# A transformer block on one core: weighted values ahead of scores in two steps, another order of GpSimd's last groups, x transposes one by one, more banks for the last group

## What is computed

```
qkv = x @ w_qkv.T + b_qkv                       # x is [4, 512, 512]
scores = q @ k.T / sqrt(32) + causal            # per head
out = softmax(scores) @ v
x = layernorm(x + out @ w_out.T + b_out)
W = (w_int - 128) * scale                       # gate, up, down
h = silu(x @ Wg.T) * (x @ Wu.T)
x = layernorm(x + h @ Wd.T)
```

## Time and profile before

| | us |
|---|---|
| median of 3 runs | 764.74 (764.24 to 765.97) |
| profiled execution | 766.57 |
| its span, first to last instruction | 764.4 |

### The profile page before, as it was taken

One profiled execution on the slowest core, in us unless ns is written; L12 is line 12 of the kernel. 1 busy time (PEld: TensorE's weight loads), 2 busy tenths in 40 slices (PEclk: granted clock), 3 DMA queues, 4 the chain that ended last, 5 costly groups with the idle time before them and its releaser, 6 DMA issues.

```text
span 764.4 us, 11953 instructions
## 1 busy us (share of the span) xinstructions
PE 739.4 (97%) x4480; PEld 567.4 (74%) x4480; DVE 393.2 (51%) x1004; ACT 382.7 (50%) x912; POOL 135.6 (18%) x154
## 2 busy tenths in 40 slices
PE   7999899999999999999799999999999999999995
PEld 6776676776776677776478887888887888788884
DVE  3757566566666665676643222553226432363335
ACT  3656767666767666766646565322323222322230
POOL 0000111314221151300736222220000000000003
PEclk9999999999999999999999999999999999999998
DMA  9201422334531355211586964541110011000201
GB/s 318 95 1 29 138 64 75 83 85 110 166 84 56 83 153 158 50 56 56 127 145 145 200 226 138 167 138 41 69 56 0 9 51 49 0 1 27 83 1 57
DMA packets 59463, 68.67 MB, mean 90 GB/s; under 512 B 33552, under 2 KB 35600, under 8 KB 59280
## 3 DMA queue, kind: packets, MB, share of 16 engines
q1 hardware_dynamic: 52880, 48.00, 20.7%
q0 software_dynamic: 6528, 19.93, 11.1%
HBM read 59.53 MB, written 14.68 MB: 97 GB/s over the span
## 4 chain that ended last, share of the span: by engine, by line
PE 90%; DVE 4%; POOL 3%; ACT 2%; DMA 1%; issue 0%; POOLq 0%; SPq 0%; DVEq 0%
PE bank L1425 15%; PE bank L1424 15%; PE bank L1210 12%; PE bank L1286 9%; PE bank L1431 7%; PE bank L1432 7%; PE bank L1225 6%; PE bank L1269 5%; PE bank L1244 5%; PE bank L1307 5%; DVE probs L968 1%; POOL z_tok L643 1%; PE bank L1318 1%; PE bank L1182 1%; PE bank L1172 1%; PE bank L1393 1%
## 5 line engine op out<-in xcount | busy, mean ns | idle before, releaser
L752 ACT ACTIVATE probs<-probs,neg_max 128x128 f32<-128x128 f32 (+3 forms) x256 | 140.4, 553 | 12.2 <-DVE neg_max L968 12.2
L1084 DVE SCALAR_TENSOR_TENSOR hid<-bank,u_scale,silu 128x512 f32<-128x512 f32 x64 | 48.0, 751 | 166.9 <-PE bank L1425 165.7
L968 DVE CUSTOM_DVE_ANT_0 probs<-bank,causal 128x128 f32<-128x128 f32 (+3 forms) x256 | 111.7, 484 | 29.4 <-PE bank L1269 28.2
L1424 PE MATMUL bank<-xT_hi,gateT 128*128 128x512 f32 x256 | 100.3, 392 | 0.0
L1425 PE MATMUL bank<-xT_lo,gateT 128*128 128x512 f32 x256 | 99.7, 389 | 0.0
L1424 PE MATMUL bank<-xT_hi,upT 128*128 128x512 f32 x256 | 99.6, 389 | 0.0
L1425 PE MATMUL bank<-xT_lo,upT 128*128 128x512 f32 x256 | 99.6, 389 | 0.0
L860 ACT ACTIVATE silu<-bank,g_scale 128x512 f32<-128x512 f32 x64 | 44.0, 687 | 99.6 <-PE bank L1425 99.6
L804 ACT ACTIVATE probsT<-bank 128x512 f32<-128x512 f32 x80 | 47.7, 597 | 90.0 <-PE bank L1286 89.8
L1286 PEld LDWEIGHTS bank<-ident,probs 128*128 128x128 f32 x640 | 73.3, 141 | 26.1 <-issue 15.4
L1431 PE MATMUL bank<-downT,hid_hi 128*128 128x512 f32 x232 | 90.6, 390 | 0.9 <-DVE hid_lo L1088 0.8
(11 more groups left out here) (102 smaller groups left out, 1165.3 us busy)
## 6 DMA issues: line engine op xcount, KB each, us to landing
scan_buf<-in_L_ffn_gate_w_dram SPq DMA_DIRECT2D x4, 1024.0 KB, 5.1
scan_buf<-in_L_ffn_up_w_dram SPq DMA_DIRECT2D x4, 1024.0 KB, 5.0
scan_buf<-in_L_ffn_down_w_dram SPq DMA_DIRECT2D x4, 1024.0 KB, 5.0
x_tok<-y_scratch SPq DMA_DIRECT2D x4, 1024.0 KB, 6.1
w_int<-in_L_ffn_gate_w_dram POOLq DMA_DIRECT2D x16, 256.0 KB, 3.5
w_int<-in_L_ffn_up_w_dram POOLq DMA_DIRECT2D x16, 256.0 KB, 2.9
w_int<-in_L_ffn_down_w_dram POOLq DMA_DIRECT2D x16, 256.0 KB, 3.8
z_tok<-y_scratch SPq DMA_DIRECT2D x4, 1024.0 KB, 5.6
```

Source lines behind the costliest of these rows:

```text
L752: nc.scalar.activation(probs[qb][:, j, :], probs[qb][:, j, :], ACT.Exp, bias=neg_max[:, qb, j:j + 1], scale=-1.0, accum_out=row_sum[:, qb, ...
L968: nc.vector.tensor_tensor_reduce(out=probs[qb][:, j, :], in0=score[j][:, first:first + w], in1=causal[:, S - w:S], scale=-SCALE, scalar=-F ...
L1084: nc.vector.scalar_tensor_tensor(out=hid[:, i % 2, :], in0=bank[:, :], scalar=u_scale[:, i:i + 1], in1=silu[:, i % 2, :], op0=ALU.mult, op ...
L1424: nc.tensor.matmul(acc[n][:, :], w[:, c, cols], form(xT_hi[:, c, :]), start=c == 0, stop=False)
```

## The change

Seven things change.

1. **Order within two steps.** At a step with scores, the weighted values go first: at step 0 the last two products of the group before, at step 8 the first two. Scores and transposes follow.
2. **x tiles.** From the second batch on they are transposed at steps 1, 2, 5 and 6, in the first at 2, 4, 5 and 6; `counts` is changed to fit.
3. **Last group.** At step 5 the output projection of tokens 2 and 3 (`EARLY`) is begun, in work banks: two groups' heads of each (6 matmuls each), then the third (3 each), with a wait for `att_ready` at each. From then on transposes have the score banks too (7 banks in `Banks`).
4. **POOL.** The bias of the last batch is added in group 14, the stores of batch 2 move behind `att_lo(14)`.
5. **Feed-forward, first batch.** Turn 0 uses banks 0 and 1, turn 1 banks 2 and 3, turn 2 waits for one product less.
6. **Feed-forward, exact weights.** A transposed tile no longer waits for the widening of a weight piece.
7. **Feed-forward, batches 1 and 2.** Four of the eight down matmuls of turn 13 move behind the gate and up matmuls of turn 15.

```diff
-    X_STEPS = [4, 4, 6, 6]
+    X_STEPS = [1, 2, 5, 6]
+    X_FIRST = [2, 4, 5, 6]
...
     EVEN = [8, 0, 0, 4, 0, 4, 8, 0, 6, 0, 6, 0, 6, 0, 0, 6]
+    AMONG_X = [4, 4, 0, 4, 0, 4, 8, 0, 6, 0, 6, 0, 6, 0, 0, 6]
...
-            return [("k", 3)] + ahead, [8, 0, 0, 4, 0, 0, 0, 0, 6, 0, 6, 0, 6, 0, 0, 6]
+            return [("k", 3)] + ahead, [8, 4, 0, 0, 0, 0, 0, 0, 6, 0, 6, 0, 6, 0, 0, 6]
...
+            if G == GROUPS - 1 and s == OUT_STEP:
+                for t in EARLY:
+                    banks.start(("o", B - 1, t))
+                banks.count = WORK + HG
...
-        score, work, pv_acc = bank[0:HG], bank[HG:HG + WORK] + bank[0:QH], bank[HG + WORK]
+        score, work, pv_acc = bank[0:HG], bank[HG:HG + WORK] + bank[0:HG], bank[HG + WORK]
...
-            return 1 if i == 0 else 0
+            return 1 if i == 1 else 0
...
+                if g == 2 and b == LAST:
+                    add_bias(LAST)
                 if G == GROUPS - 1:
+                    store_third()
                     choose_path()
...
-                if g == 2 and b == LAST:
-                    for t in range(NT):
-                        pool.wait_ge(y1_done, (LAST - 1) * NT + t + 1)
-                        nc.gpsimd.dma_start(y1_v[LAST - 1][:, t, :], z_tok[:, t, :]).then_inc(third_stored, 16)
...
-            add_bias(LAST)
...
+                    for m in products_at(STEPS) if s == 0 and G > 0 else ():
+                        weighted_values(G - 1, m)
                     if s in SCORE_STEPS:
+                        for m in products_at(s):
+                            weighted_values(G, m)
...
-                        for t in range(QH):
-                            pe.wait_ge(max_done, (G * NT + NT - 1) * HG + t + 1)
-                            for _ in range(MM - 3):
-                                next(outs[t])
+                        for heads in (2, 1):
+                            for t in EARLY:
+                                for _ in range(3 * heads):
+                                    next(outs[t])
...
-                    if n >= 2:
+                    if n < 2:
+                        wait_at_rest(WORK + 2 + n)
+                    if n >= 2 and (not short or PIECES[n - 2][0] == "y"):
                         pe.wait_ge(*piece_evicted(PIECES[n - 2], order))
...
+                        if ahead and i == NI - 2:
+                            pe.wait_ge(hid_ready, b * NI + i)
+                            down_tiles(b, i - 1, range(QH))
+                            continue
+                        if ahead and i == NI - 1:
+                            down_tiles(b, i - 2, range(QH, NT))
```

More of the change, by code:

```diff
@@ L105, in filling @@
             return ([("v", b + 1, 0), ("v", b + 1, 1)] + ahead, EVEN) if b < LAST else ([], [0] * STEPS)
[L106 to L113, removed]
+        before = [("o", b - 1, t) for t in range(QH, NT)]
+        return (before + ahead, AMONG_X) if b < LAST else (before, AMONG_X[:8] + [0] * (STEPS - 8))
     def tasks_at(s):
@@ L121, in x_at @@
     def x_at(G, s):
-        return [t for t in range(NT) if X_STEPS[t] == s] if G % NG == 2 else []
+        return [t for t in range(NT) if (X_STEPS if G > NG else X_FIRST)[t] == s] if G % NG == 2 else []
     FILLING = [filling(G) for G in range(GROUPS)]
@@ L136, in postln_block_kernel, with start @@
     PLACE = {}
-    OUT_STEP = 5
+    OUT_STEP, EARLY, LATE = 5, (QH, QH + 1), (0, 1)
     class Banks:
         def __init__(self):
-            self.uses, self.ended, self.busy, self.now = [0] * WORK, list(range(-WORK, 0)), {}, 0
-        def start(self, job):
-            free = [i for i in range(WORK) if i not in self.busy.values()]
+            self.uses, self.ended, self.busy, self.now = [0] * (WORK + HG), list(range(-WORK - HG, 0)), {}, 0
+            self.count = WORK
+        def start(self, job, among=None):
+            free = [i for i in among or range(self.count) if i not in self.busy.values()]
             i = min(free, key=lambda n: self.ended[n])
@@ L181, in postln_block_kernel @@
             banks.part(jobs, sum(counts[:s]), counts[s])
-    for t in range(QH):
[L183 to L186, removed]
+    for t in LATE:
+        banks.start(("o", B - 1, t), [i for i in range(WORK + HG) if i not in (WORK, WORK + 1)])
+    for t in range(NT):
         banks.end(("o", B - 1, t))
@@ L1161, in bank_for, with wait_at_rest @@
                     pe.wait_ge(work_drained[i], n)
+                elif i >= WORK:
+                    pe.wait_ge(max_done, (GROUPS * NT - 1) * HG + i - WORK + 1)
                 return work[i]
+            def wait_at_rest(i):
+                pe.wait_ge(work_drained[i], banks.uses[i])
             def full_of(*job):
@@ L1364, in _ @@
                         transpose_inverse(G)
-                    for m in products_at(STEPS) if s == 0 and G > 0 else ():
-                        weighted_values(G - 1, m)
-                    for m in products_at(s):
+                    for m in products_at(s) if s not in SCORE_STEPS else ():
                         weighted_values(G, m)
@@ L1374, in _ @@
                 weighted_values(GROUPS - 1, m)
-            for t in range(QH, NT):
+            for t in LATE:
                 for _ in range(MM - 3):
@@ L1443, in down @@
                                 wait_drained(pe, "o", B - 1, t)
+                            for n in range(WORK):
+                                wait_at_rest(n)
                             pe.wait_ge(normed, GROUPS)
@@ L1449, in down, with down_tiles @@
                         return
-                    for t in range(NT):
+                    down_tiles(b, i, range(NT))
+                def down_tiles(b, i, tiles):
+                    for t in tiles:
                         last = down_block(b, i, t)
-                    last.then_inc(down_full, 1)
+                        if t == NT - 1:
+                            last.then_inc(down_full, 1)
                 pe.wait_ge(max_done, GROUPS * NT * HG)
@@ L1460, in ffn @@
                 for i in range(NI):
-                    if i == 1:
-                        for t in range(QH):
-                            wait_drained(pe, "o", B - 1, t)
-                    if i >= 2:
+                    if i < 2:
+                        wait_at_rest(WORK + 2 * i)
+                        wait_at_rest(WORK + 2 * i + 1)
+                    if i == 2:
+                        pe.wait_ge(hid_done, 1)
+                    if i > 2:
                         pe.wait_ge(hid_done, i)
-                    if i == 0 and not short:
+                    if i == 1 and not short:
                         pe.wait_ge(*piece_evicted(PIECES[n - 1]))
@@ L1469, in ffn @@
                     gate_up(0, i, first_bank(i), lambda c: [wait_drained(pe, "x", B, t) for t in range(NT)] if c == 0 else None)
[L1470 to L1471 removed]
+                    if i == 1 and not short:
+                        pe.wait_ge(hid_done, 2)
                     for piece in pieces_at(i)[:-1]:
```

13 lines of the change are left out of this document (7 added, 6 removed).

## The result

The changed kernel takes 754.4 us (median of 4 runs, 753.84 to 755.36), the kernel before on the same chip 764.5; the ratio is 0.987, 95% interval 0.984 to 0.991. Timed again beside the later experiments (e11) it took 754.92 (5 runs, 754.19 to 755.28; ratio 0.987, 0.985 to 0.989). It is faster by 1.3%, 3.3 to 3.8 us above the forecast of 751.1: outside the forecast's own range of 749 to 753.5, inside the range of 8 in 10 (747.5 to 756.5). The median lies between rivals B (753.5) and A (756.2), so the time alone doesn't tell them from the forecast; the trace has to. The profiled execution took 754.66 us.

A forecast was written before the change was run, and what follows sets the result against it. PE, busy 739.4 of 764.4 us, was taken to set the time. Gains of 4.2 + 1.2 + 0.5 + 5.3 + 2.4 = 13.6 off 764.7 gave 751.1 us, own range 749 to 753.5, 8 in 10 747.5 to 756.5.

The forecast's parts named there:

- rival B: Feed-forward outruns its weights, ACT and PE stall 1 to 3 us, with other new waits this size: 753.5, chance 0.17.
- Rival A: The swap pays nothing, since scores behind values cost what projections behind values do: 756.2 us, chance 0.15.
- part 3: End of attention: stores moved behind the low part, 12 matmuls ahead of the wait, no clock fall: 5.3 us (2.8 to 6.3).
- Part 1: Weighted values first in 30 places, 4.28 to 4.08 us each; 21 places summed here: 4.2 us (0 to 7.4).
- does an earlier neighbour now wait?: Check of the swap: six projections and four transposes still cover DVE's copy; about 0.2 us of wait in groups 6, 10.
- the 0.2 of wait for tasks 5 and 6: Groups 6 and 10: tasks 5 and 6 come 0.8 us nearer to tasks 3 and 4, about 0.2 us of wait.
- Part 2: x tiles moved to single steps: groups 6 and 10 gain 1.2 us (0 to 2.9), group 2 0.5 (-1.5 to 2).
- the 0.5 of wait that was left: End of attention: PE, with 12 matmuls done at 377.6, still waits 0.5 us for POOL's low part.
- The 0.8 for the maxima: End of attention: PE's 0.8 us of waiting for the row maxima was to go.
- Part 4: Feed-forward: waits for `gateT` (0.6) and `hid_lo` (0.8) go, with 1.0 of late starts: 2.4 us (1.4 to 2.5).
- Rivals C: Slower: the clock falls in every group at tasks 5 and 6, 1.8 us each; 778 us, chance 0.04.
- D: It does more: transposes behind scores cost 0.87 and x waits vanish; 746.2 us, chance 0.06.

The follow-up runs named there:

- e11: The changed kernel itself, unchanged, timed once more beside the later experiments: 754.92 us.
- e2: Changed kernel with the old order (scores, transposes, values) at steps 0 and 8 of groups 1 and 2 alone: 754.37 us.
- e6: Changed kernel with the old steps of x and of the projections in group 2 and the old order in group 1: 752.36 us.
- e1: Kernel before with the swap alone, weighted values ahead of the scores in all 30 places: 760.6 us.
- e9: Changed kernel with the second product of step 8 between the third and fourth projection in 13 groups, two switches more: 758.53 us.
- e10: Changed kernel with the old order in group 1 and group 2's x tiles at steps 3, 4, 5 and 6: 751.24 us.
- e4: Kernel before with POOL's order alone changed, bias ahead of group 14's widening and four stores behind the low part: 760.24 us.
- e8: Changed kernel with 6 instead of 12 output projection matmuls ahead of the wait for group 14's low part: 756.31 us.
- e7: Changed kernel with feed-forward turns 14 and 15 of batches 1 and 2 as before: 756.39 us.
- e3: Changed kernel with the order scores, values, transposes, projections at steps 0 and 8: 755.05 us.

## Why the prediction was right in most of its mechanisms and 3.5 us low

**The starting point: wrong reading.** The prediction set the span of the profiled execution, 764.4, beside the median of the runs, 764.7, and called the profile 0.3 below the median. The two don't compare: around the span lie 2.2 us (766.57 less 764.4; 754.66 less 752.6 in the changed kernel), so the profiled execution was 1.8 above the median then known and 2.4 above that of 39 runs. It was a run with two falls of the clock. Terms that include falls, 1.8 in part 3 and the gain in group 2, were taken off a median that holds about one. Taken off 766.6, the same 13.6 would have given 753.0, so about half of the 3.5 us lies here, and most of the other half in group 1 (below). The profiles differ by 11.8 us, the medians by 9.5 (764.2 against 754.7, the median of nine runs), and runs at a clock of 0.996 or more by about 7.7 (761.9 against 754.2). Most of that can be added up: 11.8 less the two falls (1.25 and 1.5) and the 0.9 of group 0 is 8.15.

**Part 1, the swap: right, but for group 1.** The place came to 4.08 us, as forecast, the nine regular groups to 3.4 against 3.6. Rival A is out. The step that failed is "does an earlier neighbour now wait?": it looked at groups 6 and 10 and took the six projections as cover. Group 1 has none at step 8 and three at step 9; there the values themselves, 0.79 us behind the transposes, had covered DVE's copy of task 3, and now stand ahead of them. In place of the +0.4 stand -1.1, of which some 0.7 are these steps, with a wait that was not there:

```profile
63.75 0.63 PE L1182 MATMUL bank<-ident,w_stage 128*128 128x128 f32 x4 [0.68 <-DVE probsT L479]
```

At step 0 the values, now first, wait for DVE's copy of v (`PE bank L1317 <- DVE v_tok L964: 0.2, 1, 0.2` in the waits of the changed kernel, in none of the kernel before), and with it 0.2 more is lost there, where 0.2 was to be gained. The prediction had looked at waits that the values had in their old place. e2 and e6 show it: with the old order in group 1 the 1.1 came back. Groups 6 and 10 did as forecast (1.1 against 1.2, of which e1 shows 0.7 for the swap, so 0.4 for the x steps); the 0.2 of wait for tasks 5 and 6 that was set down for them is too short for the list of waits, but it is there: the chain of group 6 (under e9) has PE's transposes begin at 180.05, when DVE's copy of task 3 has ended. The two come 1.0 us nearer by the rows (3.4 less 2.4), not 0.8.

**Part 2, group 2: sign right, size wrong.** It gained 0.1 instead of 0.5, inside the bounds, but by luck: only since the fall of the clock that the profile before had there was missing in the profile after. Without falls on either side the new steps cost 1.5 us against the old (e6 against the changed kernel), 2.0 against e10. The prediction named the mechanism, "ACT comes to its weight copy only behind tile 0 and two exponentials", and set the waits "as large" as before. The step not taken was to follow it on: ACT would wait 2.3 us for the tile, and on DVE four rows of maxima stand behind the weight's low half.

**Part 3, the end of attention: 5.0 against 5.3.** The stores gave 2.3 (e4), the twelve matmuls 1.2 (e8), the fall 1.5 instead of 1.8 (e4). The low part ends at 373.9 us, when the twelfth matmul ends, so the 0.5 of wait that was left is 0. The 0.8 for the maxima went at the output matmuls, but a wait of 0.6 for them is new at the scores of step 3. It comes with the swap, not from the other: e1 has both (0.8 and 0.6), e4 only the first. More banks for the last group were tried by no run alone. In the medians the 1.5 counts only for the runs that had the fall.

**Part 4, feed-forward: 2.4, as forecast**, 1.4 of it by the split (e7). Rival B is out: SP issues the second chunk until 399.9 us, ACT's first use of it is at 404.4, and no staged weight is among the waits. What rival B named beside it, new waits of this size elsewhere, did come: the 3.8 us in groups 1 and 2.

**Rivals C and D.** The clock did not fall in every group: in the nine regular groups every profile with the swap (but for e9) gains the same to 0.1 us. The falls seen lie in groups 2, 14 and 15, the places where, but for the first loads, PE waits longest. D, 0.35 a place, is out: transposes behind scores take 1.02.

## What to carry to other kernels

A block that is moved ahead takes its cover with it. For each of its old places look at what stands behind it, above all in the groups whose filling differs from the rest: one such group cost 1.1 us here, a third of what the swap gained in nine others. When a tile moves earlier on one engine, follow every engine that copies it, in list order, to the first thing that PE needs. And before gains are taken off a median, compare the profiled execution's own time with it, not its span, and see which stretches at a lower clock it holds that other runs may not.

## What the runs showed of the hardware

- A switch between blocks that use 32 rows, 32 columns or the whole array costs about 0.15 us on average: two switches 0.32 in one place, 0.29 a group (e9); the same four blocks take 4.08 us in both orders with three switches (changed kernel, e3) and 4.28 in the one with four. It is shown for the pairs of these orders, not for every pair. The Trainium skill (TensorEngine Tiling (Array Packing), Key Properties) has a change of tiling mode drain the engine; the runs fit that and add the price.
- The clock falls in one execution and not in the next of the same program, with waits ahead of it that the trace shows alike (e11): around the same two waits of 1.1 and 1.0 us in group 14 it fell in six of eleven profiles. In the kernel before, a fall cost 1.25 us in group 2 and 1.5 at the end of attention, in the changed kernel 1.4 in group 14 (e11); 30 of 39 runs of the kernel before had a mean clock below that of the fastest nine. A single profile can show a cost that the median run has only in part.
